# Preparing both 77-key attentions beside the attention ahead of each, in a two-layer decoder on one core

## The reference

```
L0: latent attention (causal, 16 heads of 64)      -> "first attention", stage L0a
    cross attention on ctx, 16 heads of 16,
      layernormed q and k, rotary on q             -> "second attention", stage L0x, kind "rope"
    expert choice over 8 experts, capacity 2       -> stage ec
L1: self attention with a relative bias            -> "fourth stage", L1a, kind "t5"
    cross attention on ctx, no norms or rotary     -> "fifth stage", L1x, kind "cross"
    self attention and a top-2 mixture of experts  -> stages L1s and moe
```

## Time and profile before

| what | value |
|---|---|
| three runs | 2058.86, 2063.77, 2051.85 us (median 2058.86) |
| the profiled execution | 2055.67 us, span 2053.7 us |
| PE busy | 1769.1 us (86%) |
| DVE, ACT, POOL busy | 1146.3 (56%), 1007.1 (49%), 737.8 (36%) |
| first attention, about | 0 to 326 us |
| second attention, about | 326 to 575 us |
| expert choice, about | 575 to 890 us |
| fourth stage, about | 890 to 1309 us |
| fifth stage with the self attention | from 1309 us |

### The profile page before, as it was taken

How to read it: one execution, slowest core, us unless ns; L and a number is a source line. 1 busy time by engine, 2 the same in 40 slices (tenths; PEclk the granted TensorE clock), 3 DMA queues, 4 the chain that set the end, 5 groups by cost and what they waited for, 6 DMA issues and landing times. The chain is left out here.

```text
span 2053.7 us, 40778 instructions
## 1 busy us (share of the span) xinstructions
PE 1769.1 (86%) x15132; PEld 1414.8 (69%) x15132; DVE 1146.3 (56%) x3110; ACT 1007.1 (49%) x2377; POOL 737.8 (36%) x651
## 2 busy tenths in 40 slices
PE   6889874888849999959999999688899968699994
PEld 5777664666538888847777777566577747588883
DVE  3656664356446464636566665355478743257774
ACT  5555551355325454526555555255456633156663
POOL 2334342677322424123333333212234530614442
PEclk9999997799669999979999999799789988899997
DMA  2000002000062524230000000201004119213334
GB/s 69 12 12 22 12 7 80 1 16 23 22 227 83 164 83 123 93 87 2 11 12 11 12 12 6 72 17 55 27 7 137 43 35 363 100 46 52 52 52 103
DMA packets 93673, 121.25 MB, mean 59 GB/s; under 512 B 8458, under 2 KB 80602, under 8 KB 93450
## 3 DMA queue, kind: packets, MB, share of 16 engines
q1 hardware_dynamic: 80186, 100.89, 14.9%
q0 software_dynamic: 13296, 17.77, 5.0%
HBM read 82.94 MB, written 37.80 MB: 59 GB/s over the span
## 5 line engine op out<-in xcount | busy, mean ns | idle before, releaser
L2022 POOL TENSOR_TENSOR L1a_probs<-L1a_probs,L1a_rinv 128x1024 f32<-128x1024 f32 x64 | 121.3, 1895 | 217.9 <-DVE L1a_rinv L2337 217.9
L2019 POOL TENSOR_TENSOR L0a_probs<-L0a_probs,L0a_rinv 128x256 f32<-128x256 f32 (+1 forms) x128 | 103.2, 828 | 186.0 <-DVE L0a_rinv L2337 186.0
L3015 POOL DMA_INDIRECT moe_sums<-moe_y,moe_xg x39 | 83.6, 2144 | 158.4 <-DVE moe_y L3314 145.9
L2329 DVE CUSTOM_DVE_ANT_0 L1a_sbias<-L1a_psS,L1a_bias 128x256 f32<-128x256 f32 x256 | 93.2, 421 | 81.4 <-PE L1a_psS L2129 81.4
L2612 POOL DMA_INDIRECT ec_sums<-ec_yk,ec_token_at x32 | 61.9, 1934 | 190.0 <-ACT ec_yk L2737 184.8
L2280 ACT ACTIVATE L1a_probs<-L1a_sbias,L1a_nmx 128x256 f32<-128x256 f32 x256 | 126.3, 498 | 1.5 <-DVE L1a_nmx L2329 1.5
L2280 ACT ACTIVATE L0a_probs<-L0a_sbias,L0a_nmx 128x128 f32<-128x128 f32 (+1 forms) x256 | 112.8, 443 | 28.9 <-DVE L0a_nmx L2329 28.9
L2799 DVE TENSOR_TENSOR ec_h<-ec_sg,ec_psU 128x512 f32<-128x512 f32 x64 | 43.9, 686 | 120.1 <-ACT ec_sg L2720 120.1
L3093 PE MATMUL moe_psY<-moe_wts,moe_hT 128*128 (+1 forms) x440 | 105.9, 384 | 5.5 <-ACT moe_hT L3160 3.4
L2045 PEld LDWEIGHTS L1a_psF<-L1a_xT,ec_wt 128*128 128x128 f32 x756 | 92.4, 190 | 25.9 <-issue 17.9
L2045 PE MATMUL L1a_psF<-L1a_xT,ec_wt 128*128 128x256 f32 x756 | 104.8, 288 | 4.4 <-DVE L1a_xT L2354 4.4
(11 more groups left out here) (593 smaller groups left out, 4948.7 us busy)
## 6 DMA issues: line engine op xcount, KB each, us to landing
shelf<-in_L_ffn_w_gate SPq DMA_DIRECT2D x8, 1024.0 KB
shelf<-in_L_ffn_w_up SPq DMA_DIRECT2D x8, 1024.0 KB
ec_wd<-in_L_ffn_w_down SPq DMA_DIRECT2D x8, 1024.0 KB, 6.1
moe_rows<-blank SPq DMA_DIRECT2D x1, 5070.0 KB, 19.9
moe_xg<-moe_rows SPq DMA_DIRECT2D x39, 130.0 KB
moe_wts<-in_L_ffn_e_gate SPq DMA_DIRECT2D x8, 512.0 KB, 10.1
moe_wts<-in_L_ffn_e_up SPq DMA_DIRECT2D x8, 512.0 KB, 9.9
moe_wts<-in_L_ffn_e_down SPq DMA_DIRECT2D x8, 512.0 KB, 10.1
```

The costliest lines, as they stand in the source:

```text
L2019: last = pool.tensor_tensor(v, v, bcast(rinv[:, r, :, t], 2, KEYS[t]), ALU.mult)
L2022: last = pool.tensor_tensor(v, v, bcast(rinv[:, r, :, :].rearrange("p h t -> p (h t)"), 2, S), ALU.mult)
L2329: last = dve.tensor_tensor_reduce(out=sbias[:, g % 2, j, at], in0=psS[:, slot + j, at], in1=added, scale=-1.0, scalar=LARGE, op0=ALU.add, ...
L3015: pool.indirect_dma_start(sums, bass.IndirectOffsetOnAxis(ap=xg[:, j % RX, D:D + 1].bitcast(U32), axis=0), y[:, j % RY, :], None, compute_ ...
```

## The change

A new function `context_early` takes the loads and the preparation out of `context_stage`. It allocates the tiles that hold them (on the right side of SBUF for the second attention, on the left for the fifth stage), and returns five generators, of which TensorE's is empty. `wide_stage` takes these as `beside` and calls `next` on them at hooks. `context_stage` gets the tiles and semaphores as `early`. What is prepared early: high and low halves of q's, k's and v's weights (not the output's), masks, and for the second attention the centring, bias rows, tables and columns. What is loaded early: weights, biases, tables, contexts, and for the second attention its first five inputs, which are outputs of the host. Low halves for the second attention move from VectorE to GpSimd. The `qk` tile of the fourth stage shrinks from 16 slots to 3.

```diff
+def context_early(nc, name, kind, x_in, w, gate_w, side):
...
+    def sync_program(sp):
+        sp.dma_start(raw[:, :, 0:D], w["wq_t"]...).then_inc(q_in, 16)
+        sp.dma_start(raw[:, :, D:3 * D], w["wkv_t"]...).then_inc(kv_in, 16)
+        yield
+        if rope:
...
+        yield
+        sp.dma_start(cb[:, 0:CT - 1, :], flat[0:(CT - 1) * P, :]...).then_inc(c_in, 16)
...
+        sp.dma_start(raw_o[:], w["wo_t"]...).then_inc(o_in, 16)
+        yield
+        if rope:
+            for b in range(RX - 1):
+                sp.dma_start(xb[:, b, :, :], x_in[b, :, :, :]).then_inc(x_in_sem[b], 16)
+                yield
+    def scalar_program(act):
+        for n, j in enumerate((0, 1) if rope else (1, 0)):
+            act.wait_ge((q_in, kv_in)[j], 16)
+            if rope:
+                act.wait_ge(w_centred, n + 1)
+                act.activation((wq, wk)[j][:, 0, :, :], src, ACT.Copy).then_inc(w_high, 1)
...
+            yield
+        act.activation(wv[:, 0, :, :], raw[:, :, 2 * D:3 * D], ACT.Copy).then_inc(w_high, 1)
+    def gpsimd_program(pool):
+        if rope:
+            for j in range(2):
+                pool.wait_ge(w_high, j + 1)
+                pool.tensor_tensor((wq, wk)[j][:, 1, :, :], raw[...], (wq, wk)[j][:, 0, :, :], ALU.subtract)
+                yield
+            pool.wait_ge(w_high, 3)
+            pool.tensor_tensor(wv[:, 1, :, :], raw[:, :, 2 * D:3 * D], wv[:, 0, :, :], ALU.subtract)
+        yield
+    def vector_program(dve, ident):
...
+        set_masks(dve, ident)
+        yield
+        if rope:
+            for j in range(2):
+                dve.wait_ge((q_in, kv_in)[j], 16)
...
+                wstep(dve.tensor_reduce(m, wide, AX_X, ALU.add))
+                yield
+                wstep(dve.tensor_scalar(m, m, -1.0 / HD, None, ALU.mult))
+                dve.tensor_tensor(wide, wide, bcast(m, 3, HD), ALU.add).then_inc(w_centred, 1)
+                yield
+            set_row(0)
+            yield
+            set_row(1)
+            yield
+            dve.wait_ge(small_in, 16 * 6)
+            set_tables()
+            yield
+            set_columns()
+        else:
+            for n, j in enumerate((1, 0)):
+                dve.wait_ge(w_high, n + 1)
+                dve.scalar_tensor_tensor(out=wqk[:, 1, :, j, :], in0=raw[...], ..., op1=ALU.subtract)
+                yield
+            dve.wait_ge(w_high, 3)
+            dve.tensor_tensor(wv[:, 1, :, :], raw[:, :, 2 * D:3 * D], wv[:, 0, :, :], ALU.subtract)
...
 context_stage, SyncE:
-            load_x(0)
-            (all loads of weights, rows, tables, contexts, output weights)
+            if not rope:
+                for b in range(RX - 1):
+                    load_x(b)
...
 context_stage, VectorE:
             if rope:
-                centre(0)
-                set_row(0)
-                low_qk(0)
                 take(("xT",), 0)
-                centre(1)
-                set_row(1)
-                dve.wait_ge(small_in, 16 * 6)
-                set_tables()
                 spread_q(0)
-                set_masks()
-                set_columns()
                 for n in range(3):
                     take(("cT", n), 0)
-                low_qk(1)
                 turn_pairs(dve, 0)
...
 wide_stage:
-            qk = sb("qk", [P, 2, NP, 2, S])
+            qk = sb("qk", [P, 3, 2, S])
...
+        POOL_HOOKS, ACT_HOOKS, DVE_HOOKS = (30, 34, 38), (28, 32, 36), (range(16, 34, 2) if latent else (30, 34, 38, 42))
...
                 sp.dma_start(x_out[b, :, :, :], xn[:]).then_inc(x_stored, 16)
                 sp.wait_ge(x_stored, 16 * (b + 1))
+                next(tail, None)
+            for _ in tail:
+                pass
...
 at the end of each engine's turn of the loop over g:
+                if g in DVE_HOOKS:
+                    next(tail, None)
+            for _ in tail:
+                pass
...
 attention_stage:
+    if kind != "self":
         consts[6].append((name, kind, x_in, x_out, w))
+        return
+    latent, rope, choice, biased, cross = consts[6]
+    early, beside = context_early(nc, rope[0], rope[1], rope[2], rope[4], a["L0_ffn_gate_w"], "right")
+    wide_stage(nc, latent[0], latent[1], consts, *latent[2:], beside)
+    held = expert_choice_run(nc, consts, choice[2], a, rope, early, biased[4])
+    early, beside = context_early(nc, cross[0], cross[1], cross[2], cross[4], None, "left")
+    wide_stage(nc, biased[0], biased[1], consts, *biased[2:], beside, held)
+    context_stage(nc, cross[0], cross[1], consts, *cross[2:], early, follow=...)
```

More of the change, by code:

```diff
@@ L115, in context_stage @@
+def context_stage(nc, name, kind, consts, x_in, x_out, w, early, aff=None, follow=None):
     ident = consts[0]
@@ L170, in context_stage @@
         if rope:
[L171 to L183, removed]
+            wq, wk, rows, same, cross, shift_q, kn_masked, gate = (
+                early[k] for k in ("wq", "wk", "rows", "same", "cross", "shift_q", "kn_masked", "gate"))
             qc = sb("qc", [P, 2, TT, H, HD])
@@ L834, in _ @@
             if rope:
-                take(("xT",), 0)
-                high_qk(0)
-                for what, b in FRONT[1:6]:
-                    take(what, b)
-                    if what == ("q", 1):
-                        high_qk(1)
-                        high_v()
-                for what, b in FRONT[6:]:
+                for what, b in FRONT:
                     take(what, b)
@@ L845, in _ @@
             else:
-                for j in range(3):
-                    take(*FRONT[j])
-                high_qk(1)
-                take(*FRONT[3])
-                high_qk(0)
-                high_v()
-                for what, b in FRONT[4:]:
+                for what, b in FRONT:
                     take(what, b)
@@ L2128, in scores @@
                         else:
-                            last = pe.matmul(psS[:, slot + j, t * S:(t + 1) * S], qk[r, b % 2, p, 0, rows],
-                                             qk[r, b % 2, p, 1, :], start=True, stop=True)
+                            last = pe.matmul(psS[:, slot + j, t * S:(t + 1) * S], qk[r, g % 3, 0, rows],
+                                             qk[r, g % 3, 1, :], start=True, stop=True)
                 last.then_inc(s_ready, 1)
@@ L2214, in _ @@
         def _(act):
+            tail = beside.scalar(act)
             def split(dst, src, scale=1.0):
@@ L2307, in _ @@
                     apply_input(b + 1)
+                if g in ACT_HOOKS:
+                    next(tail, None)
+            for _ in tail:
+                pass
             take_out(G - 2)
@@ L2312, in _ @@
         def _(dve):
+            tail = beside.vector(dve, ident)
             def set_bias(heads):
```

299 lines of the change are left out of this document (146 added, 153 removed).

## The result

On one chip, in the same session, the changed kernel took 2049.27 us in the median of 20 runs (2039.30 to 2056.44) and the kernel before 2054.75 us (20 runs, 2043.24 to 2063.77). The medians are 5.5 us apart. The ratio is 0.9968, 95% interval 0.9955 to 0.9982: by it 6.6 us faster, with 3.7 to 9.2 as the bounds. That is a real gain but under 0.5%, so by the bound set in the prediction it counts as "same". The time lies in the forecast range; the gain is half of the forecast 13.9. Two repeats agree: 0.9953 (0.9934 to 0.9971) on that chip, and 0.9972 (0.9953 to 0.9992) on another one, where both kernels are about 25 us quicker.

A forecast was written before the change was run, and what follows sets the result against it. It took waits where stages meet as the bound, TensorE being busy 86% of the span. -12.2 + 0.4 - 5.8 + 3.7 = -13.9 gave 2041.8 from the profile, 2045.0 from the median; forecast 2044 us, range 2036 to 2053.

The forecast's parts named there:

- Second attention's front: Start of the second attention up to its first scores: inputs and preparation already there, first scores 12.2 us earlier.
- Rival B: Second attention: GpSimd's queue keeps the pace after the first scores, gain only 9.2 us in sum, 2049.7 us; chance 0.15.
- Seam: Between first and second attention: SyncE issues the fifth input load after the last store, ahead of the barrier, +0.4 us.
- Fifth stage's front: Start of the fifth stage: contexts ready at once, input 3.4 us later, its load hidden; 5.8 us saved.
- Rival A: Second attention: denser front keeps the clock up (-3.5 us), host work all hidden (-3.7 us), 2037 us; chance 0.2.
- First attention as host: First attention's loop: hooked preparation for the second attention costs 3.7 us, between 0 and 9.5.
- Pairs 16, 24 and 32: First attention, hooks at index 0, where VectorE's gap is used up: pieces paid whole, 2.8 us.
- the collision: First attention, pair 30: GpSimd's subtract and VectorE's tables come together, 0.6 us added, half of GpSimd's 1.27.
- Rival D: Hooks run late, behind the loop, their work paid whole at the host's end: -9.4 us in sum, 2049.5; chance 0.06.
- Fourth stage: Host for the fifth stage's preparation: four hooks in VectorE's waits cost 0, at most 2.7 us.
- rival C: Second attention's steady part falls to a lower clock; at 0.76 it eats the 13.9 us gain; chance 0.04.
- One sign of being wrong: First attention: the prediction counts as wrong if this stage loses over 10 us.

The follow-up runs named there:

- index0: The changed kernel with VectorE's nine hooked pieces done in threes behind pairs 16, 24 and 32 of the first attention: 2052.07 us, ratio to before 0.9978.
- again: The changed kernel run once more, unaltered: 2048.88 us (11 runs), ratio to the kernel before 0.9953.
- before3: The kernel before, unchanged, profiled a third time: 2033.71 us in one run.
- again2: The changed kernel, unaltered, for a third profile and more rounds: 2024.23 us (12 runs), ratio to the kernel before 0.9972.

## Why the prediction was half right

*Second attention's front, forecast -12.2.* Right. From the stage's start: q's projection at 2.5 (forecast 2.6), GpSimd's root of q 8.6 (9.0), k's projection 9.8 (10.3), root of k 14.0 (14.5), right behind q's, first scores 19.1 (19.9). The forecast chain is the real one, and the mean front is 12.8 us shorter than in the three profiles of before. Rival B, the front given back behind the first scores, falls: the rest of the stage took 199.2 to 203.1 us with an early front, 200.0 to 204.3 without.

*Seam, +0.4.* Right: 3.2 to 3.6, and 3.2 again when the load is issued before the wait.

*Fifth stage's front, -5.8.* Right in its chain (contexts at once, input 3.4 later, load hidden), too small by 0.5 to 1.4: 15.4 or 14.5 to 8.2. Here the clock rises 7 to 14 us earlier. Rival A had this mechanism, but in the second attention. There the clock rose 10 us earlier too (6 to 7 us into the stage, not 17), yet the rest of the stage shows under 1 us of it.

*First attention as host, +3.7.* This is the term that was too small: 5.5, 7.0 and 6.7. The prices of the pieces themselves were good. Pairs 16, 24 and 32 cost 0.64, 0.83 and 1.30, together 2.77 where the prediction has 2.8; the tables with the collision 1.22 where it has 0.9; everything else 0.1: 4.1 in sum. The collision alone cost 1.1 where the prediction has 0.6, the tables 0.1 where it has 0.3. The difference is that the prediction ended a hook's price at the piece's own length. When a piece lengthens TensorE's wait (to 2.60 us in the profile after, to 2.18 in `index0`), the clock can fall behind it, and the matmuls of a pair or two run at half rate: 1.4 to 2.9 us more in the three profiles, 6 in `index0`. Where it fell besides pair 31 changed from profile to profile (behind pair 25 or 33, or nowhere). The wait was there to be read in the earlier trace rows, 1.38 us ahead of the values already, and the block put 1.1 on top. Rival D (hooks late, work at the end) falls, each piece ran at its pair; that its 2049.5, like B's 2049.7, meets the median is chance.

*Fourth stage, 0, and ring of three, 0.* Right to 0.4 us in 418: its four hooks cost no pair anything.

*The sum.* Corrected with what the profiles show of the code, fronts first: -12.8 + 0.4 - 7 + 6.4 + 0.4 = -12.6, close to the forecast 13.9. Measured by the ratios: -6.6, -9.7 and -5.7. What is left, 3 to 7 us, is at least as much as the host term was short by (2.7), and its cause stays open. In the one profile of the changed kernel whose time lies near its median, `again`, the whole difference from the first profile of before is -5.9; there the first attention up to pair 16 and its end bring +7.7 and the self attention +1.3, all in unchanged code. But `before3` loses as much at that start and end, and `again2` nothing. Two of the three profiles of the changed kernel (after and `again2`) were its fastest executions, so the profiles flatter it. The prediction's rival C named a loss by the clock in unchanged code, with one place and 13.9 us as its size; what came is smaller and not in that place.

*The time.* The forecast 2044 was counted from three runs with the median 2058.86; all 20 runs have 2054.75. From there the forecast gain leads to 2040.9, and 2049.27 is 8.4 us above it. That the time lies well inside the range owes 4.1 us to that baseline, which is luck.

*The signs.* One sign of being wrong did appear in part: the first attention's last store came 14.7 us later in `again` than in the first profile of before, more than the 10 allowed, though only 6.1 later than in `before3`. The three profiles of before differ by 8.6 there among themselves, nearly as much as the bound.

*Chances.* 0.72 for faster by over 0.5% was too much. The fronts were forecast within 1.4 us, but the 13.9 stood only 3.6 us beyond the bound, and host and clock were known to act against it.

## What to carry to other kernels

Work moved beside a loop is free only where the engine that takes it waits for another that is busy all that time. Look in the list of waits for the long ones (here 5.2 us on average, eight times), not for the average, and place the work ahead of such a wait, after whatever the critical engine needs next: the same 8.2 us cost 14 us in threes at index 0, 5.5 to 7 singly at every second pair, and 0 in threes one pair behind index 0. If a moved piece lengthens a wait of TensorE (here from 1.5 to 2.6 us), count with the matmuls of the next pair or two at half rate as well. And compare stages over several profiles of both kernels before a difference of a few us is put down to the change.

## What the runs showed of the hardware that I had not expected

- The clock falls in one execution and not in the next at the same place of the same code: the last 48 matmuls of the output projection, with 0.98 us of idle ahead each time, took 5.98 us in before, 8.47 in `before3` and 7.47 in after.
- A wait of 2.6 us, where the kernel has 1.51 without the block, was followed by matmuls at half rate in four profiles of four (8 matmuls in 1.2 to 1.55 us, not 0.87).
- A 128x16 operation of VectorE on two SBUF tiles took 1.25 us and not 0.17 beside a GpSimd operation of 1.27: what the block cost went by the other engine's instruction, not by its own.
- Over 80% of the variance of the time between runs of the kernel before goes with the mean clock: 1.5, 1.6 and 1.8 us for 0.001 (28, 23 and 17 runs).
- Two chips differ by 1.2% with the same kernel (2054.4 and 2030.2 us), nearly all of it in the last stage, the experts (357 to 362 us on one, 335 to 337 on the other), while every other stage agrees to within what profiles of one chip scatter.
